# A four-layer graph network on one core: variance about one step's mean, a dealt-out opening block, and layer rows made during the gathers

## The reference, cut to what matters

```
h = relu(layernorm(x)); x = x + leaky(nb @ W1.T + b1 + (h*nb) @ W2.T + b2)    nb = segment_sum(w * h[src], dst)
h = relu(layernorm(x)); x = x + h + norm(f)          f = gelu(mean_nb(h) @ Wl.T + bl + h @ Wr.T)
h = relu(layernorm(x)); x = x + mean_cliques @ W.T + b
h = relu(layernorm(x)); x = x + GRU(h, segment_sum(m[src], dst)) @ Wout.T + bout
norm(f): out = f - mean_scale*mean(f);  out / sqrt(mean(out*out) + eps) * gn_weight + gn_bias
```

## Time and profile before

| | us |
|---|---|
| median of 3 runs | 2127.67 (2126.10 to 2128.21) |
| the profiled execution | 2126.4 |
| its span | 2124.5 |
| outside the span | 1.9 |
| PE busy | 1960.0 (92%) |
| DVE busy | 1495.2 (70%) |
| ACT busy | 1213.0 (57%) |
| POOL busy | 143.0 (7%) |

### The profile page before, as it was taken

How to read it: one execution, slowest core, us unless ns; L and a number is a source line. 1 busy time by engine, 2 the same in 40 slices (tenths; PEclk the granted TensorE clock), 3 DMA queues, 4 the chain that set the end, 5 groups by cost and what they waited for, 6 DMA issues and landing times.

```text
span 2124.5 us, 62668 instructions
## 1 busy us (share of the span) xinstructions
PE 1960.0 (92%) x22393; PEld 1770.5 (83%) x22393; DVE 1495.2 (70%) x3079; ACT 1213.0 (57%) x3193; POOL 143.0 (7%) x120
## 2 busy tenths in 40 slices
PE   1289999999999999999998999999998878999997
PEld 1279999999999999999998777777887867888854
DVE  8588888888888888888885666666886457000066
ACT  5376666666666666666663888888996643000042
POOL 4700000000000000000000000000000053000021
PEclk7589999999999999999999999999999989999999
DMA  8331222222222222222224333333686169988722
GB/s 234 92 126 71 102 76 101 81 96 87 89 93 83 100 76 102 74 102 74 102 74 142 136 132 131 131 131 131 215 314 223 52 213 356 368 305 301 263 72 75
DMA packets 184485, 304.21 MB, mean 143 GB/s; under 512 B 12641, under 2 KB 135958, under 8 KB 184174
## 3 DMA queue, kind: packets, MB, share of 16 engines
q1 hardware_dynamic: 180506, 290.74, 38.9%
q0 software_dynamic: 3904, 12.50, 1.9%
HBM read 202.70 MB, written 100.48 MB: 143 GB/s over the span
## 4 chain that ended last, share of the span: by engine, by line
PE 82%; ACT 5%; DVE 4%; issue 3%; DMA 3%; POOL 1%; DVEq 1%; ACTq 1%; SPq 0%; POOLq 0%
PE ps L907 26%; PE ps L999 21%; PE ps L896 11%; PE ps L890 7%; PE ps L991 6%; PE ps L977 3%; PE ps L1188 2%; ACT edge_area L1355 1%; PE ps L1066 1%; POOL edge_area L728 1%; PE ps L1163 1%; DMA hs<-node_rows 1%; PE ps L1074 1%; ACT edge_area L1293 1%; ACT big L1361 1%
## 5 line engine op out<-in xcount | busy, mean ns | idle before, releaser
L1355 ACT CAST edge_area<-ps 128x392 f16<-128x392 f32 x784 | 408.1, 520 | 392.9 <-PE ps L890 392.9
L907 PE MATMUL ps<-big,rows_area 128*128 128x128 f32 x4802 | 577.0, 277 | 0.0
L907 PEld LDWEIGHTS ps<-big,rows_area 128*128 128x128 f32 x4802 | 551.9, 192 | 0.0
L896 PE MATMUL ps<-edge_area 128*128 128x98 f16 x6272 | 418.9, 209 | 0.0
L1361 ACT COPY big<-ps 128x392 f32<-128x392 f32 x784 | 418.0, 533 | 0.5 <-PE ps L896 0.3
L1859 DVE TENSOR_TENSOR edge_area<-lo_pair,carry 128x1024 f16<-128x1024 f16 x392 | 276.5, 705 | 133.2 <-PE ps L896 131.9
L896 PEld LDWEIGHTS ps<-edge_area 128*128 128x128 f16 x6272 | 333.2, 98 | 0.0
L890 PE MATMUL ps<-edge_area 128*128 128x98 f16 x3136 | 277.4, 210 | 27.6 <-DVE edge_area L1865 14.3
L999 PE MATMUL ps<-big,agg 128*128 128x256 f16 (+1 forms) x2450 | 278.8, 271 | 0.0
L999 PEld LDWEIGHTS ps<-big,agg 128*128 128x128 f16 x2450 | 232.3, 98 | 25.6
L890 PEld LDWEIGHTS ps<-edge_area 128*128 128x128 f16 x3136 | 190.4, 98 | 44.4 <-DVE edge_area L1865 17.3
(11 more groups left out here) (256 smaller groups left out, 1754.2 us busy)
## 6 DMA issues: line engine op xcount, KB each, us to landing
big<-edge_counts SPq DMA_DIRECT2D x315, 448.0 KB, 5.2
edge_counts<-edge_area SPq DMA_DIRECT2D x49, 1568.0 KB, 5.5
agg<-edge_counts SPq DMA_DIRECT2D x21, 448.0 KB, 6.5
hs<-node_rows POOLq DMA_DIRECT2D x14, 448.0 KB, 4.3
edge_area<-x_stream SPq DMA_DIRECT2D x14, 448.0 KB, 4.0
node_rows<-rows_area SPq DMA_DIRECT2D x1, 3136.0 KB, 13.0
agg_s<-node_rows SPq DMA_DIRECT2D x49, 64.0 KB, 4.8
agg_s<-in_x SPq DMA_DIRECT2D x49, 64.0 KB, 1.8
```

The source lines that it names most:

```text
L896: last = mm(pair_of(p_weight[s % 4], c), sources_of(slot, r, c), cells_of(oh, slot, r, c), start=(c == 0 and oh is oh_whi), stop=(c == 3 a ...
L907: last = mm(p_sum, h0[:, n, :], w32[:, par, n, :], start=(n == 0), stop=(n == NB - 1))
L1355: nc.scalar.copy(store_slot[:, par, :, cols], p_count[s % 2]).then_inc(sem("count_taken"), 1)
```

## The change

1. **Layer 0's rows.** POOL makes none. ACT makes rows 0 to 12 before the first group of records is in and rows 13 to 29 before the second; DVE makes rows 30 to 41 and 42 to 48 in the same two places. `row_scales` and `row_shifts` move ahead of `keys(0)`, and ACT's square root ahead of `high_parts(0)`.
2. **Tail and block 0.** The pieces of block 0 are loaded while the last `weigh` frees their buffer, not after it; block 0's cliques are loaded at the start of counting and split while DVE waits in the tail. One `p_reach` sum goes ahead of the last `lin1`. Block 0 is dealt out: four `products`, then for each piece its flip, up to three further `products`, and the mix of the piece before. ACT counts four pieces before it copies flips; DVE counts all seven before its first `add_mix`.
3. **Layer 1.** Two buffers each for rows, transposed rows and neighbour means; transposes go to pA and pD in turn; ACT copies transposed rows. The mean of step 0 is the centre. Each step is centred and squared as soon as its Gelu is done; DVE adds the 7 blocks of a step before PE sums over partitions (2 products instead of 14) for steps 0 to 4; mean and variance come from the centred sums at the end. All loops are written out.

```diff
-ACT_ROWS = 24
+ACT_ROWS = (13, 30)
+DVE_ROWS = (42, NB)
# POOL
-            for b in range(ACT_ROWS, NB):
-                nc.gpsimd.tensor_scalar(h0[:, b, :], h0[:, b, :], rstd0[:, b:b + 1], shift0[:, b:b + 1], ALU.mult, ALU.add)
...
# ACT
+            nc.scalar.activation(rstd0, rstd0, ACT.Sqrt).then_inc(sem("ln_std"), 1)
+            act.wait_ge(sem("ln_scaled"), 1)
+            h0_rows(0, ACT_ROWS[0])
             act.wait_ge(sem("w_scale_ready"), 1)
             high_parts(0, *TILES[0])
...
+            h0_rows(*ACT_ROWS).then_inc(sem("h0_ready"), 1)
             high_parts(1, *TILES[1])
# DVE
+            row_scales()
+            row_shifts()
+            dve.drain()
+            h0_rows(ACT_ROWS[1], DVE_ROWS[0])
             keys(0, *TILES[0])
-            row_scales()
             low_weights(0, *TILES[0])
-            row_shifts()
+            h0_rows(*DVE_ROWS).then_inc(sem("h0_ready"), 1)
# SP, tail of counting
+                for k in range(4):
+                    sp.wait_ge(sem("piece_used"), k + 1)
+                    load_piece(0, 0, k)
                 store_x(NB - 2, 1)
...
-                sp.wait_ge(sem("agg_done"), 1)
-                load_cliques(0, True)
-                for k in range(SUBS):
-                    load_piece(0, 0, k)
# PE, block 0
+                    for k in range(FIRST_PIECES):
+                        block_products(k)
+                    for k in range(SUBS):
+                        flip(k, k, 0, 2)
+                        if k + FIRST_PIECES < SUBS:
+                            block_products(k + FIRST_PIECES)
+                        if k:
+                            mix(k - 1, (k - 1) % 2, 0, 0, 2, used=True)
# PE, layer 1
+            for i in range(1, NS):
+                if i + 1 < NS:
+                    rows_T(i + 1)
                 lin2(i)
+                if i == 1:
+                    mm(pC[:, 0:D], ones[:], block_sums[1][0], start=True, stop=True).then_inc(sem("sums_made"), 1)
+                if i > 2:
+                    sum_blocks(i - 3)
+            sum_rows(NS - 2)
+            sum_blocks(NS - 3)
+            sum_rows(NS - 1)
# ACT, layer 1
+            for i in range(NS):
                 gelu(i)
+                if i + 2 < NS:
+                    stage_agg(i + 2)
+                    copy_rows(i + 2)
+                if i > 0:
+                    square(i - 1)
# DVE, layer 1
+            def over_step(out, rows):
+                return V.tensor_reduce(out, rows.rearrange("p b d -> p d b"), AX_X, ALU.add).then_inc(
+                    sem("rows_summed"), 1)
...
+            for i in range(2, NS - 1):
+                add_bias(i)
+                centred(i - 1)
+                sum_steps(i - 2)
+            add_bias(NS - 1)
+            centred(NS - 2)
+            centred(NS - 1)
+            sum_steps(NS - 3)
```

More of the change, by code:

```diff
@@ L60 @@
 IN_ODD = 3
+FIRST_PIECES = 4
 SPLIT_AT = 3
@@ L1022, in multiply_block @@
                         products(par, k, width).then_inc(sem("piece_used"), 1)
[L1023 removed]
+                        if cliques:
                             if k == 0:
[L1025 removed]
+                                mix(n - 1, (par + 1) % 2, b - 1, 1 - par, 2, used=first)
                             else:
@@ new lines, in lin2, with sum_blocks, sum_rows @@
+                product(pB, [(agg_pair[i % 2], wt["WlT"][:]), (hT_pair[i % 2], wt["WrT"][:])]).then_inc(sem("lin2"), 1)
+            def sum_blocks(i):
+                for n in range(2):
+                    pe.wait_ge(sem("rows_summed"), 2 * i + n + 2)
+                    mm(pC[:, n * TILE:n * TILE + D], ones[:], block_sums[i % 2][n], start=(i == 0), stop=False).then_inc(
+                        sem("sums_made"), 1)
+            def sum_rows(i):
+                for n, (rows, made) in enumerate(((f_all, "centred"), (sq_all, "squared"))):
+                    pe.wait_ge(sem(made), i + 1)
+                    for b in range(i * SB, (i + 1) * SB):
+                        k = LAST if b == NB - 1 else P
+                        last = mm(pC[:, n * TILE:n * TILE + D], ones[0:k, :], rows[0:k, b, :], start=False, stop=(b == NB - 1))
+                    last.then_inc(sem("sums_made"), 1)
@@ L1320, in take_table, with h0_rows @@
                 from_tab(lambda t, v: nc.scalar.copy(t, v), tabs[tab], *TILES[n], side).then_inc(sem(f"tab_taken{side}"), 1)
+            def h0_rows(first, last):
+                for b in range(first, last):
+                    done = nc.scalar.activation(h0[:, b, :], h0[:, b, :], ACT.Relu, bias=shift0[:, b:b + 1],
+                                                scale=rstd0[:, b:b + 1])
+                return done
+            act.wait_ge(sem("ln_var"), 1)
+            nc.scalar.activation(rstd0, rstd0, ACT.Sqrt).then_inc(sem("ln_std"), 1)
+            act.wait_ge(sem("ln_scaled"), 1)
+            h0_rows(0, ACT_ROWS[0])
             act.wait_ge(sem("w_scale_ready"), 1)
@@ L1334, in _ @@
             order = act.value_load(any_order[0:1, 0:1], min_val=0, max_val=1)
-            def h0_rows(first, last):
-                for b in range(first, last):
-                    done = nc.scalar.activation(h0[:, b, :], h0[:, b, :], ACT.Relu, bias=shift0[:, b:b + 1],
-                                                scale=rstd0[:, b:b + 1])
-                if last == ACT_ROWS:
-                    done.then_inc(sem("h0_ready"), 1)
-            def h0_all():
-                act.wait_ge(sem("ln_scaled"), 1)
-                h0_rows(0, ACT_ROWS)
             def take_supergroup(h, par, i, s):
@@ L2117, in take_block @@
                             last.then_inc(sem("piece_counted"), 1)
-                            if cliques and not (first and k == 0):
-                                add_mix(b * SUBS + k - 1, (k + SUBS - 1) % SUBS, first)
+                            if cliques and not first:
+                                add_mix(b * SUBS + k - 1, (k + SUBS - 1) % SUBS)
                             if split and k == SPLIT_AT:
                                 split_cliques(b + 1, 1 - par)
+                        if first:
+                            for k in range(SUBS - 1):
+                                add_mix(k, k, True)
                         dve.drain()
```

354 lines of the change are left out of this document (204 added, 150 removed).

## The result

The changed kernel takes 2092.94 us (median of 4 runs, 2090.85 to 2094.66) against 2127.94 us (4 runs, 2126.1 to 2129.68). The ratio is 0.9836, 95% interval [0.9822, 0.985]. 35.0 us are gone; 41.6 were forecast (2086 us, range 2075 to 2098). The profiled execution took 2094.1 us with a span of 2092.4 us.

The account below looks back on a forecast made before the run. TensorE, carrying 82% of the chain of waits, was taken as the bound. Profiled 2126.4 us less 12.0, 6.4 and 23.2 gave 2084.8; with the median 1.3 above the profiled execution, 2086 us, range 2075 to 2098.

Parts of the forecast that it names:

- Part 1: Layer 0's rows in the opening: first weigh at 120.0 against 133.25, 13.3 us less 1.3, so 12.0 us gained.
- The 1.3 us given back: Opening: 1.0 us for gathers held up by VectorE's new row work, 0.3 for ScalarE's lateness.
- Rival C: Opening: VectorE's row operations block gathers for their whole length, up to 7 us instead of 1.0; 2092 us, chance 0.07.
- ScalarE's cover: Opening: ScalarE's 17 rows take 6.6 to 7.6 us in its idle time before 80.25, 0 to 0.7 us late.
- Part 2: Tail and block 0: TensorE starts sooner after the branch, block 1's first flip at 1189 against 1195.38; 6.4 us gained.
- the gap: TensorE's idle time after the branch before block 0, read as code loading behind piece loads: 2.5 us instead of 6.91.
- Rival A: Tail: the gap after the branch stays 6.9 us, not the pieces' doing, leaving 0.5 us gain; 2092 us, chance 0.12.
- Part 3: Layer 1: TensorE paces steps at 4.45 us, square root at 1679.9 against 1705.12, 2 us given back; 23.2 us gained.
- rival D: Layer 1: strided reductions slow, VectorE pacing from 4.3 us each; slower than before, 2130 us at 4.5; chance 0.03.
- Rival B: Layer 1: copies and Gelu swap ScalarE's tables in each step, 7.8 us in all; 2094 us, chance 0.07.
- E: Layer 1: step stays at 5.85 us by hand-overs between engines, only the serial pass shortens; 2091.5 us, chance 0.09.
- From the square root to `new_x` nothing changes: Behind layer 1's square root: the stretch to `new_x` stays at 8.5 us, the shift being carried to the end.

Follow-up runs that it names:

- rows_alone: The kernel before with only the layer-row part (rows made by ScalarE and VectorE during the gathers): 2121.61 us, ratio 0.9968.
- two_parts: The changed kernel with the old variance (two passes over all rows behind the last step): 2111.26 us, ratio 0.9919 to the kernel before.
- side_by_side: The changed kernel with layer 1's step sums reading seven neighbouring numbers instead of seven 512 bytes apart: 2087.53 us, a single run.
- changed_third: The changed kernel unaltered, run a third time as base for later kernels: 2092.07 us, ratio 0.983 to the kernel before.
- pool_centres: The changed kernel with the centring of steps 0 to 4 on GpSimd: 2105.26 us beside the changed kernel's 2106.71 on the same chip.
- six_late: The changed kernel with the second stage's first six piece loads behind GpSimd's first block: 2104.16 us beside the changed kernel's 2106.71 on the same chip.
- both: The changed kernel with the edits of pool_centres and six_late together: 2104.01 us beside the changed kernel's 2106.71 on the same chip.

## Why the prediction was right, and where it was not

Distance to the kernel before in the profiled executions, in us:

| place | rows_alone | two_parts | changed | side_by_side | forecast |
|---|---|---|---|---|---|
| start of layer 1 | 12.1 | 18.4 | 17.7 | 17.6 | 18.4 |
| square root | 12.3 | 18.4 | 37.8 | 41.0 | 41.6 |
| first new rows summed | 10.0 | 16.2 | 35.4 | 38.7 | 41.6 |
| end of the long product | 6.7 | 14.3 | 34.3 | 37.4 | 41.6 |
| first products of the last stage | 6.7 | 14.3 | 34.0 | 37.1 | 41.6 |
| end of the span | 1.2 | 11.9 | 32.1 | 38.7 | 41.6 |

**Part 1, forecast 12.0.** 12.1 at the start of layer 1, and that it fits so closely is luck. The one-hot of 0.69 us and the weigh within 0.5 us of 120.0 came as worked out. The 1.3 us given back did not: I had put them at the gathers and at ScalarE's lateness, so ahead of the first weigh, and there nothing is lost (13.5 us at the weigh, 13.3 forecast before the give-back). As much is lost elsewhere, for which the prediction has no term: 0.7 us bit by bit over the 48 halves that follow (12.8 us at the last weigh) and 0.7 in block 0. Rival C (gathers blocked) did not happen: the longest gather under VectorE's new row operations is 1.11 us against 0.95 (1.60 on chip Y). ScalarE's cover was worked out as 0 to 0.7 us late and came out 0.31 to 0.75 us early on X; that on another chip the tables could be 12.6 us late, and the rows then stand on the path, no part of the prediction had.

**Part 2, forecast 6.4.** Added to part 1 it is worth 6.3 (two_parts against rows_alone). But inside one trace, from the last weigh to block 1's first flip, it is 4.1 (changed, 17.75 - 13.6) to 4.4 (two_parts): the gap came out at 2.9 to 3.6 us instead of 2.5, and from TensorE's start to block 1 it took 29.0 to 29.3 us instead of 28.0. The other 2 us are what rows_alone loses on the way there and these two don't. So parts 1 and 2 are right as a sum, 17.7 to 18.4 against 18.4, by an error in each that the other makes good. The mixes' waits are 0.4 to 0.6 as said. Rival A did not happen, since the gap did not stay at 6.9; its price was not consistent either, as the part's own terms leave 2.0 us with an unchanged gap, not 0.5. That transfers in flight lengthen the gap is supported by fourteen traces and not separated from the code's place.

**Part 3, forecast 23.2.** This is the step that failed: "No row shows a reduction with such a stride; the nearest is 1.19 us for 1024 elements [...] I take 1.05". It measures 1.70 to 1.73. VectorE then needs 5.25 us a step and becomes the pace in TensorE's place, and the stage is worth 20.0 us to the square root. side_by_side, which differs in the stride alone, gives 23.4 (68.50 - 45.10): with the price I took, the term would have been right. The mechanism was named as rival D, with the place right and the size wrong by far: D lets VectorE pace the layer from 4.3 us a reduction on. By the prediction's own terms it does so from (4.45 - 2 x 1.01) / 2 = 1.2 us on, the upper end of the range it gave, and at 1.70 to 1.73 it did. (The part's timeline also adds up to 1680.2, not 1679.9, and eleven strided reductions run, not thirteen; neither matters here.) Rival B is out (one table load), and E too: the step tightened from 5.85 until VectorE stopped it. The Trainium skill (Advanced Engine Details and Errata, "Memory Cachelines") says that accesses which go to another 16-byte line each time are slower; that is the rule I should have weighed. The trace agrees, with 1.73 against 1.08 us at a stride of 512 bytes; this section of it gives no factor, and from which distance on the cost is paid no run here shows.

**Behind the square root, forecast 0.** The second failure: "From the square root to `new_x` nothing changes" holds to 0.5 us in the changed kernel (1.4 in side_by_side), but I stopped there. GpSimd's add waits 4.10 us in every trace but the one of before; the stretch from the square root to the first summed rows takes 12.8 to 13.2 us in all of them and took 10.5 before, so 2.3 us and more of the wait reach the path. Waits for pieces of the second stage, with the DMA share near 1 from 1711 to 1770, then take back 0.5 to 3.3 us. In two of the traces, changed and changed_third, the first products of the last stage ran at the lower clock (0.64 granted from 1980 to 1984 in changed; 3.35 and 2.99 us instead of 1.77); why in these two, no trace says. In the changed kernel that is 2.3 + 1.1 + 0.3 + 1.7 of the 5.7 us, and rows_alone and two_parts show that the first two of these meet every kernel that comes earlier.

In the profiled executions 9.5 us are missing at the end (41.6 - 32.1): 3.8 up to the square root, 3.4 of them the stride's, and 5.7 behind it. In the medians it is 6.9 (2092.9 against 2086), because the profiled execution after lies 1.2 us above its median and that of before 1.3 under the median that the forecast was made from.

## What to carry to other kernels

Price a reduction by its access pattern as well as its count: the same 896 f32 elements took 1.08 us side by side and 1.73 us at 512 bytes apart, and where two of them sit in a loop that is nearly balanced, that decides which engine paces it. Work put into an engine's idle time is free only by the slack that is left (here 0.3 to 0.75 us of 7.4); look for an idle stretch that nothing waits behind, as ScalarE's 9.9 us were. And follow a gain to the end of the span: 12 to 41 us earlier at the square root, the kernels here lost 2.8 to 5.5 us again before the long product was done, at GpSimd's wait and at the pieces. When GpSimd and VectorE work at the same time, look in the trace at which of them starts first: in the last stage 0.1 us of order decides over 1.7 us of a step.

## What the runs showed of the hardware

- VectorE, 128x128 from 128x896 f32: 1.73 us with seven operands 512 bytes apart, 1.08 us with neighbours.
- GpSimd's f32 `tensor_tensor` of 128x896 takes 2.06 to 2.22 us. Beside VectorE's reductions (one input) and its bias add (one input in PSUM) neither gets longer (VectorE's 1.70 to 1.77 and 1.09 us in pool_centres).
- Beside a VectorE `tensor_tensor` with both inputs in SBUF it does: in the last stage the one that starts second waits for the other. VectorE's 1.09 us become 2.81 to 2.98, GpSimd's 2.07 become 2.67 to 3.04, by who starts first, in every step where the two overlap, in all fourteen traces.
- GpSimd's second operation of the second stage waits 4.09 to 4.10 us in thirteen traces, with a DMA share of 0.21 as with 1.0, with 75 more instructions ahead of it or none, with a semaphore wait ahead of it or none; and 0.84 in the kernel before, the only one in which GpSimd had made rows earlier. In later steps of the same stage it waits 0.24 to 0.62 us (up to 4.5 in six_late and both, where the pieces load during these steps). A cost that falls due once, at GpSimd's first use of something, and that the rows of the opening had paid would fit; no run tests it, and the cause is open.
- During the gathers ScalarE waited 9.0 to 10.6 us at its first table copies on chip Y, in all four traces there, and 0.3 us on X; the changed kernel ran on both.
